# Beginning the first feed-forward group inside the attention's last pair

## The reference, cut to what matters

```python
def _L0_ffn_ref(x, W_fc, W_proj):
    h = jnp.square(jax.nn.relu(jnp.einsum('bsd,fd->bsf', x, W_fc)))
    y = jnp.einsum('bsf,df->bsd', h, W_proj)
    ...   # five steps of a membrane; the spikes are counted
    return jnp.sum(spks, axis=0) / NUM_STEPS
...
x = x + jnp.tanh(g_xattn[0]) * _L0_xattn_ref(ctx_1024, _layernorm(x, axis=-1), mask, ...)
x = x + jnp.tanh(g_ffn[0]) * _L0_ffn_ref(_layernorm(x, axis=-1), L0_ffn_W_fc, L0_ffn_W_proj)
x = x + jnp.tanh(g_xattn[1]) * _L1_xattn_ref(_layernorm(x, axis=-1), ctx_1024, ctx_1024, ...)
x = x + jnp.tanh(g_ffn[1]) * _L1_ffn_ref(_layernorm(x, axis=-1), ...)
```

## Time and profile before

| | |
|---|---|
| three runs | 892.55, 895.89, 898.25 us; median 895.89 |
| the profiled execution | 897.6 us, its span 895.8 us |
| busy in the span: PE, DVE, ACT, POOL | 812.0, 549.6, 368.2, 375.6 us |
| mean granted clock of TensorE | 0.93 of full speed |
| attention's pairs, in the span | from about 105 to 392 us |
| feed-forward up to the last down product | to about 510 us |

### The profile page before, as it was taken

One profiled execution on the slowest core, in us unless ns is written; L12 is line 12 of the kernel. 1 busy time (PEld: TensorE's weight loads), 2 busy tenths in 40 slices (PEclk: granted clock), 3 DMA queues, 4 the chain that ended last, 5 costly groups with the idle time before them and its releaser, 6 DMA issues.

```text
span 895.8 us, 13812 instructions
## 1 busy us (share of the span) xinstructions
PE 812.0 (91%) x4270; PEld 622.5 (69%) x4271; DVE 549.6 (61%) x1173; ACT 368.2 (41%) x1175; POOL 375.6 (42%) x396
## 2 busy tenths in 40 slices
PE   6887799898999899978999889999997799999995
PEld 5555545555555455546888778888886789999994
DVE  4949676767577676457997756777765523333331
ACT  4547134544354333425433177666671022222220
POOL 7355545363546375326433434445443302222221
PEclk9989599998899799987999989999997799999998
DMA  8570000000000000009000091000000384455520
GB/s 302 188 305 1 1 0 1 1 1 1 0 1 1 0 1 1 1 1 356 1 0 1 1 336 59 12 13 13 13 18 21 98 299 166 176 176 175 174 83 2
DMA packets 31886, 67.12 MB, mean 75 GB/s; under 512 B 3103, under 2 KB 22909, under 8 KB 30813
## 3 DMA queue, kind: packets, MB, share of 16 engines
q1 hardware_dynamic: 28699, 56.17, 18.0%
q0 software_dynamic: 2560, 10.17, 3.5%
q10 hardware_dynamic: 578, 0.19, 0.1%
HBM read 54.74 MB, written 12.68 MB: 75 GB/s over the span
## 4 chain that ended last, share of the span: by engine, by line
PE 67%; DVE 17%; issue 7%; ACT 4%; POOL 3%; DMA 2%; DVEq 0%; SPq 0%; ACTq 0%; POOLq 0%
PE PS L2045 9%; PE PS L2033 9%; PE PS L1433 7%; PE PS L727 6%; PE PS L1415 6%; PE PS L1257 4%; PE PS L718 4%; PE PS L694 3%; DVE row_best L835 3%; PE PS L719 3%; PE PS L764 2%; DVE hL L1354 2%; PE PS L736 2%; PE PS L1241 2%; PE PS L747 2%
## 5 line engine op out<-in xcount | busy, mean ns | idle before, releaser
L1027 ACT ACTIVATE EX<-PS 128x512 f32<-128x512 f32 x144 | 79.1, 594 | 139.5 <-PE PS L719 134.2
L835 DVE TENSOR_REDUCE row_best<-PS 128x1 f32<-128x1024 f32 x64 | 77.8, 1221 | 48.8 <-PE PS L694 48.5
L991 POOL TENSOR_TENSOR sumP<-sumP,EX 128x1024 f32<-128x1024 f32 x32 | 75.7, 2366 | 41.8 <-ACT EX L1027 41.3
L2033 PEld LDWEIGHTS PS<-xeT,w 128*128 128x128 f32 x736 | 85.6, 192 | 4.0 <-DMA w<-in_L_ffn_W 1.7
L2033 PE MATMUL PS<-xeT,w 128*128 128x128 f32 x736 | 86.1, 275 | 2.4 <-DMA w<-in_L_ffn_W 1.5
L1615 ACT ACTIVATE pc<-PS,mx 128x77 f32<-128x77 f32 x256 | 78.9, 360 | 21.2 <-DVE mx L1512 21.2
L2045 PE MATMUL PS<-w,heT 128*128 x368 | 83.3, 379 | 1.3 <-DVE oe L1975 1.3
L2072 POOL DMA_INDIRECT out<-oe,target x23 | 23.3, 1011 | 126.0 <-DVE oe L1975 126.0
L727 PE MATMUL PS<-EX,V 128*64 128x512 f32 (+1 forms) x288 | 76.1, 646 | 0.0
L2045 PEld LDWEIGHTS PS<-w,heT 128*128 128x128 f32 x368 | 68.1, 190 | 10.0 <-issue 1.7
L1433 PE MATMUL PS<-vw,pcT 128*128 128x256 f32 (+1 forms) x320 | 72.9, 383 | 1.2 <-ACT pcT L1628 1.2
(11 more groups left out here) (283 smaller groups left out, 1718.0 us busy)
## 6 DMA issues: line engine op xcount, KB each, us to landing
w<-in_L_ffn_W SPq DMA_DIRECT2D x31, 1024.0 KB, 6.5
vw_rows<-vwn SPq DMA_DIRECT2D x2, 1232.0 KB
kwH_rows<-kwH SPq DMA_DIRECT2D x1, 2464.0 KB, 7.4
kwL_rows<-kwL SPq DMA_DIRECT2D x1, 2464.0 KB, 13.7
kwH<-kwH_rows POOLq DMA_DIRECT2D x1, 2464.0 KB, 9.8
kwL<-kwL_rows POOLq DMA_DIRECT2D x1, 2464.0 KB, 16.0
vw<-vw_rows SPq DMA_DIRECT2D x2, 1152.0 KB, 7.3
XR<-in_x SPq DMA_DIRECT2D x4, 512.0 KB, 13.4
```

The costliest lines, as they stand in the source:

```text
L835: dve.tensor_reduce(row_best[:, n % 2, t // GT, t % GT:t % GT + 1], PSf[:, 512 * at:512 * at + S], AX.X, ALU.max, negate=True).then_inc(ma ...
L991: pool.tensor_tensor(sumP[:], before, EX[:, (KT * n + c) % EB, :, :], ALU.add).then_inc(pool_summed, 1)
L1027: act.activation(EX[0:r, k % EB, i, :], PS[0:r, ST_AT + i, :], ACT.Exp).then_inc(exp_done, 1)
L2033: last = pe.matmul(PS[:, 1 + 2 * p + c // 4, c % 4 * P:c % 4 * P + P], w1[:, u, k, c * P:c * P + P], xeT[:, p, k, :], start=k == 0, stop=k ...
```

## The change

The first feed-forward group starts earlier: group 0's statistics go into pair 6 (step 5), its normalization, transposes, copy and low part into pair 7 (steps 2, 4, 4, 5), group 1's statistics, root and normalization into pair 7 too (steps 3, 5, 6). After the last values TensorE goes straight to group 0's up products. Pair 7's sums come after chunk 1, its output products after chunks 3 and 5; VectorE does the reciprocals and additions after the hL of the same chunks. TensorE waits for `proj_added` after chunk 7, GpSimd issues its DMAs after group 0's squares. Group 0 is written out ahead of TensorE's loop, which keeps groups 1 and 2. zTH and zTL lie where wprojT was. The PSUM banks of scores and values are one lower.

Two things change in every pair: `sum_rest` is split, and both halves go into the next pair's step 0, `sum_last` behind `low_parts_of` and `scale_heads` and ahead of `row_max`, `sum_both` behind it; and the second `turn_shift` of step 8 goes between the values of chunks 7 and 8, and behind rows, heads and items in the turn of the spare banks.

```diff
@@ -252,11 +252,13 @@
-    zTH = ffn.take("zTH", [P, KC, GN], F32R)
-    zTL = ffn.take("zTL", [P, KC, GN], F32R)
     relu = ffn.take("relu", [P, 4, GN])
     spikes = ffn.take("spikes", [P, GN])
     assert ffn.at <= CROSS_LOW
+    ffn = Region(TOP - FC * D)
+    zTH = ffn.take("zTH", [P, KC, GN], F32R)
+    zTL = ffn.take("zTL", [P, KC, GN], F32R)
+    assert ffn.at <= TOP
...
     CHUNKS = ((0, 512), (512, 1024))
-    MAX_AT, ST_AT, PV_AT = 0, 3, 5
-    SPARE = (2, 6, 7)
+    MAX_AT, ST_AT, PV_AT = 0, 2, 4
+    SPARE = (5, 6, 7)
+    FFN_AT = dict(stats0=(PP - 2, 5), z0=(PP - 1, 2), stats1=(PP - 1, 3), turn0=(PP - 1, 4), low0=(PP - 1, 5),
+                  root1=(PP - 1, 5), z1=(PP - 1, 6))
+    TAIL_SUM, TAIL_OUT = 1, (3, 5)
     POOL_CHUNKS = 6
...
@@ -807,8 +814,8 @@
                         row_scores(n + 1, c, MAX_AT)
                     if c in (3, 7):
                         ctx_scores(n + 1, c // 4)
-                    if c in (5, 8):
-                        turn_shift(n + 1, (c - 5) // 3)
+                    if c == 5:
+                        turn_shift(n + 1, 0)
...
                 for v, i in items_at(n, c):
                     item(v, i)
+                if (n, c) == FFN_AT["turn0"]:
+                    pe.wait_ge(max_ready, 2 * GT * PP)
+                    ffn_turn(pe, 0)
                 for done in CHUNK_OF_STEP.get(c, ()):
+                    if done == KT - 1 and n + 1 < PP:
+                        turn_shift(n + 1, 1)
                     values(n, done)
-        sums(PP - 1)
-        project_out(PP - 1, 0)
-        project_out(PP - 1, 1)
+        return {TAIL_SUM: lambda: sums(PP - 1), TAIL_OUT[0]: lambda: project_out(PP - 1, 0),
+                TAIL_OUT[1]: lambda: project_out(PP - 1, 1)}
...
-        def sum_rest(n):
+        def sum_last(n):
             dve.wait_ge(exp_done, 2 * (KT * n + KT - 1) + 2)
             dve.wait_ge(dve_summed, 3 * n + 1)
             dve.tensor_tensor(sumD[0:C], sumD[0:C], EX[0:C, (KT * n + KT - 1) % EB, :, :], ALU.add).then_inc(dve_summed, 1)
+
+        def sum_both(n):
             dve.wait_ge(pool_summed, pool_read(n, POOL_CHUNKS - 1))
             dve.wait_ge(dve_summed, 3 * n + 2)
             dve.tensor_tensor(sumD[:], sumD[:], sumP[:], ALU.add).then_inc(dve_summed, 1)
...
+                if n > 0 and c == 0:
+                    sum_last(n - 1)
                 if n + 1 < PP and c < 2 * GT:
                     row_max(n + 1, c, MAX_AT)
+                if n > 0 and c == 0:
+                    sum_both(n - 1)
...
-                if n == PP - 1 and c == 5:
+                if (n, c) == FFN_AT["stats0"]:
                     ffn_stats(dve, 0)
+                if (n, c) == FFN_AT["z0"]:
+                    ffn_z(dve, 0)
+                if (n, c) == FFN_AT["stats1"]:
+                    ffn_stats(dve, 1)
+                if (n, c) == FFN_AT["low0"]:
+                    ffn_z_low(dve, 0)
+                if (n, c) == FFN_AT["z1"]:
+                    ffn_z(dve, 1)
                 if c == KT - 2:
                     sum_first(n)
                 if n + 1 < PP and c == KT - 1:
                     keep_shift(n + 1, 1)
                 for v, i in items_at(n, c):
                     square_sums(v, i)
-            sum_rest(n)
-        ffn_z(dve, 0)
-        reciprocals(PP - 1)
-        add_out(PP - 1, 0)
-        add_out(PP - 1, 1)
+        sum_last(PP - 1)
+        sum_both(PP - 1)
+        return {TAIL_SUM: lambda: reciprocals(PP - 1), TAIL_OUT[0]: lambda: add_out(PP - 1, 0),
+                TAIL_OUT[1]: lambda: add_out(PP - 1, 1)}
 
...
+                if (n, c) == FFN_AT["root1"]:
+                    pool_root(pool, 1)
+            if n == PP - 2:
+                pool_root(pool, 0)
...
+                if (n, c) == FFN_AT["turn0"]:
+                    act.wait_ge(wfc_split, 4)
+                    ffn_copy_turned(act, 0)
...
+    def pe_ffn(pe, tail):
+
+        def group(g, last_group, tail={}):
             pe.wait_ge(g_zT_ready, g + 1)
...
+                if c in tail:
+                    tail[c]()
+            if tail:
+                pe.wait_ge(proj_added, 2 * GT * PP)
             if not last_group:
-                turn(g + 1)
+                ffn_turn(pe, g + 1)
             pe.wait_ge(h_ready, FC * g + FC)
...
-        pe.wait_ge(proj_added, 2 * GT * PP)
         pe.wait_ge(wfc_split, 4)
-        pe.wait_ge(ffn_in, 32)
-        turn(0)
-        with pe.Fori(0, NG - 1) as g:
+        pe.wait_ge(exp_done, 2 * KT * PP)
+        group(0, False, tail)
+        with pe.Fori(1, NG - 1) as g:
             group(g, False)
         group(NG - 1, True)
...
             if not last_group:
-                copy_turned(g + 1)
-        copy_turned(0)
+                ffn_copy_turned(act, g + 1)
         with act.Fori(0, NG - 1) as g:
             group(g, False)
         group(NG - 1, True)
...
         for g in range(NG):
             group(g)
+            if g == 0:
+                pool.wait_ge(proj_added, 2 * GT * PP)
+                pool_refill(pool)
+                for p in range(2):
+                    pool.dma_start(t["mark"][p], iota_low[0:1, 0:P]).then_inc(out_rows[p], 16)
             if g + 2 < NG:
                 pool_root(pool, g + 2)
...
         for g in range(NG - 1):
-            low_parts(g, range(FC))
-            z_low(g + 1)
+            for c in range(FC):
+                low_parts(g, [c])
+                if g == 0 and c in tail:
+                    tail[c]()
+            ffn_z_low(dve, g + 1)
             if g + 2 < NG:
                 ffn_stats(dve, g + 2)
...
         pool_project(pool, 0)
         pool_wfc(pool)
         pool_attend(pool)
-        pool_root(pool, 0)
-        pool_root(pool, 1)
-        pool.wait_ge(proj_added, 2 * GT * PP)
-        pool_refill(pool)
-        for p in range(2):
-            pool.dma_start(t["mark"][p], iota_low[0:1, 0:P]).then_inc(out_rows[p], 16)
         pool_ffn(pool)
         pool_cross(pool)
```

More of the change, by code:

```diff
@@ L652, in spare_uses @@
                     yield "ctx", n + 1, c // 4
-                if n + 1 < PP and c in (5, 8):
-                    yield "shift", n + 1, (c - 5) // 3
+                if n + 1 < PP and c == 5:
+                    yield "shift", n + 1, 0
                 if n > 0 and c == 1:
@@ L665, in spare_uses @@
                     yield "item", v, i
+                if n + 1 < PP and c == 8:
+                    yield "shift", n + 1, 1
         yield "sum", PP - 1, 0
@@ L1221, in layers_kernel, with ffn_turn @@
     EDGES = spike_edges()
-    def pe_ffn(pe):
-        def turn(g):
-            pe.wait_ge(g_z, g + 1)
-            for s in range(GT):
-                for k in range(KC):
-                    last = pe.transpose(PS[:, k, s * P:s * P + P], Z[:, s, k * P:k * P + P], ident[:])
-            last.then_inc(g_zT, 1)
-        def group(g, last_group):
+    def ffn_turn(pe, g):
+        pe.wait_ge(g_z, g + 1)
+        for s in range(GT):
+            for k in range(KC):
+                last = pe.transpose(PS[:, k, s * P:s * P + P], Z[:, s, k * P:k * P + P], ident[:])
+        last.then_inc(g_zT, 1)
+    def pe_ffn(pe, tail):
+        def group(g, last_group, tail={}):
             pe.wait_ge(g_zT_ready, g + 1)
@@ L1259, in group, with ffn_copy_turned @@
                 last.then_inc(y_done, 1)
-        pe.wait_ge(proj_added, 2 * GT * PP)
         pe.wait_ge(wfc_split, 4)
-        pe.wait_ge(ffn_in, 32)
-        turn(0)
-        with pe.Fori(0, NG - 1) as g:
+        pe.wait_ge(exp_done, 2 * KT * PP)
+        group(0, False, tail)
+        with pe.Fori(1, NG - 1) as g:
             group(g, False)
         group(NG - 1, True)
-    def act_ffn(act):
-        def copy_turned(g):
-            act.wait_ge(g_zT, g + 1)
-            for k in range(KC):
-                last = act.activation(zTH[:, k, :], PS[:, k, :], ACT.Copy)
-            last.then_inc(g_zT_ready, 1)
+    def ffn_copy_turned(act, g):
+        act.wait_ge(g_zT, g + 1)
+        for k in range(KC):
+            last = act.activation(zTH[:, k, :], PS[:, k, :], ACT.Copy)
+        last.then_inc(g_zT_ready, 1)
+    def act_ffn(act):
         def group(g, last_group):
@@ L1326, in ffn_z, with ffn_z_low, dve_ffn @@
         last.then_inc(g_z, 1)
-    def dve_ffn(dve):
-        def z_low(g):
-            dve.wait_ge(g_zT_ready, g + 1)
-            for k in range(KC):
-                last = dve.tensor_tensor(zTL[:, k, :], PS[:, k, :], zTH[:, k, :].bitcast(F32), ALU.subtract)
-            last.then_inc(g_zT_low, 1)
+    def ffn_z_low(dve, g):
+        dve.wait_ge(g_zT_ready, g + 1)
+        for k in range(KC):
+            last = dve.tensor_tensor(zTL[:, k, :], PS[:, k, :], zTH[:, k, :].bitcast(F32), ALU.subtract)
+        last.then_inc(g_zT_low, 1)
+    def dve_ffn(dve, tail):
         def spike(g, halves=range(2)):
@@ L1354, in low_parts @@
                 dve.tensor_tensor(hL[:, c, :], square[:, c % 4, :], hH[:, c, :].bitcast(F32), ALU.subtract).then_inc(h_low, 1)
-        z_low(0)
-        ffn_stats(dve, 1)
```

(13 more changed lines are left out.)

## The result

The changed kernel takes 888.2 us (median of 888.6, 888.1, 879.6 and 888.3), the kernel before 897.1 beside it: 0.989 of it, 95% interval 0.984 to 0.994. That is a gain of 8.9 where 22 to 23 were forecast, and the time lies above the range. The profiled execution took 888.6, its span 886.8.

A forecast was written before the change was run, and what follows sets the result against it. TensorE, far ahead in busy time, was taken to lose time idle or at low clock at the seam and starts of pairs 3 and 5. Terms -10.1 - 10.4 - 1.3 = -21.8 took 897.6 to 875.8, median 874.1; range 868 to 883.

The forecast's parts named there:

- (a): Seam between attention and feed-forward: first down product 18.6 us after the last values, for 30.4; 11.8 off.
- the clock's fall once after the sums: Seam: one-column sums expected to lower TensorE's clock once there, a loss of 1.7 us.
- wait for `proj_added` over 0.5: Seam, a sign of the forecast coming true: TensorE would have no such wait.
- the lows of h: Seam: VectorE's hL for eight chunks, 1.25 us each, covered before the down products by only 1.2 us.
- Rival 2: Seam: VectorE bounds group 0, so the seam gives 5.4 us for 10.1; time 879; chance 10%.
- (b): Work moved into pairs 6 and 7: transposes +1.0, statistics +0.4, normalization 0.3 (between 0 and 2.4); together +1.7 us.
- (c): Starts of pairs 3 and 5: keys' low parts ahead of both sums remove the gap; 5.2 us each, 10.4 together.
- (e): Second sum behind the row maximum at the other pair starts: together 0 us, between -1 and +3.
- rival 3: Pair starts: second sum behind the maximum lengthens idle, clock falls at every start; slower, 903; chance 3%.
- rival 1: Starts of pairs 3 and 5: the clock does not come back, 2.2 us for 10.4; time 882; chance 10%.
- (d): Shift's product behind the first values: chunk 7's values run in TensorE's waits for NM and the bank; 1.3 us saved.

The follow-up runs named there:

- z0_early: Changed kernel with group 0's normalization in pair 7's step 0 in place of step 2: 883.9 us, ratio 0.983.
- seam_only: Changed kernel with VectorE's order and the shift at the pair starts put back as before, seam and moved work kept: 887.2 us, ratio 0.987.
- wide_values: z0_wide with chunk 0's values ahead of the sums: 861.6 us, ratio 0.960.
- z0_seam: seam_only with group 0's normalization in pair 7's step 0: 883.7 us, ratio 0.984.
- both_first: Changed kernel with the second sum ahead of the row maximum again, both sums still behind the keys' low parts: 886.1 us, ratio 0.989.
- z0_both: both_first with group 0's normalization in pair 7's step 0: 884.1 us, ratio 0.984.
- z0_wide: z0_early with the sums' products 64 columns wide in place of one: 873.4 us, ratio 0.974.
- before_wide: Kernel before the change with the sums' products 64 columns wide, nothing else: 885.2 us, ratio 0.988.
- z0_values: z0_early with chunk 0's values ahead of the sums, one-column products kept: 869.3 us, ratio 0.966.
- seam_values: z0_seam with chunk 0's values ahead of the sums, old order at the pair starts: 886.4 us, ratio 0.989.
- wide_values_noshift: wide_values with the shift's product where it was before the change: 860.9 us, ratio 0.960.

## Why the prediction missed

**Seam (a): right, mis-sized by 1.7.** 30.44 came to 16.93, a gain of 13.5 for 11.8. (I put two output products at 2.0 together; the halves that I named make 1.85, and they took 1.13 each.) The 1.7 was the clock's fall once after the sums; with up products on both sides the clock stayed at 1.00. No wait for `proj_added` over 0.5 appeared (0.38), and the lows of h were no bound: they take 0.69 one at a time, between GpSimd's squares, not the 1.25 I carried over from a row of eight. Rival 2 is out.

**Moved work (b): the normalization was mis-sized.** I took 0.3 between 0 and 2.4; it was 2.4 of waiting and 1.7 of clock, 4.1, and 4.3 by `z0_early`. The bound from the rows was the right wait but left out what a wait costs in clock. The rule of the Trainium skill that I had weighed ("SBUF — State Buffer", "Who interferes with whom") agrees with the 5.83 us row: the operations ended with GpSimd's additions. I chose against it because TensorE had a step between, without laying the additions of pair 7 beside the moved operations, where two more of them were due. The errors of (a) and (b), -1.7 and +3.8, cancel in part, by luck: -13.5 + 1.0 + 0.4 + 4.1 = -8.0 by the changed kernel's trace, for -10.1 forecast. `seam_only` measured -9.2 to -11.3; its trace lacks the wait of 2.4.

**Starts of pairs 3 and 5 (c): right where nothing else is late.** The gaps of 2.29 and 2.43 are gone. The new order, worth 10.4 by the forecast, is worth 13.5 in `wide_values` and 17.0 with one-column products and the values first. In the changed kernel it was worth nothing (883.9 against 883.7 in `z0_early` and `z0_seam`).

**The second sum behind the maximum (e): the step that failed.** I put it at 0, between -1 and +3, counting the waits alone, and those were right: 3.0 in six places. What I did not count is what a wait of 0.5 does to the clock when one-column products follow. In the profiled execution the stretches at 1.2 GHz grew at pairs 1, 2 and 6, stayed at 6.8 and 10.1 at pairs 3 and 5, and over all seven starts they sum to 44.2, for 44.5 before. Filling the wait brought 14.6, so by that edit the term is about +15 and not 0. With it and the other terms as forecast the sum is -10.1 - 10.4 - 1.3 + 14.6 = -7.2, for 8.9 measured. The split between (c) and (e) is mine and not measured: the second sum put back ahead of the maximum (`both_first`, `z0_both`) returns 2 us or nothing, for then TensorE waits for the maximum, 12.9 in place of 6.1. What is shown is the pair of them: 10.4 forecast, 0 found, and 17.0 once chunk 0's values stand ahead of the sums. Nor does the wait cost the same each time: at pair 4 the clock stayed at 1.00 behind 0.49 of it.

This is rival 3's mechanism, which I gave 3%. I had it decide only where further falls cost more than all the rest gained, and had no case between: the falls eat (c) and the seam's gain stays. Part of rival 1 is in it too, since the clock at pairs 3 and 5 did not come back (0.60 and 0.61); its rule of the Trainium skill ("TensorE: Matmul & The Clock Gate", "What's actually happening"), that sustained activity lifts the clock, agrees with the rows in this: at the start of pair 3 two waits and sixteen one-column products from 224.88 to 228.36, and 1.2 GHz behind them. That the one-column products weigh in this is shown by `z0_wide` and `before_wide`; that the wait does, by `z0_values` with `seam_values` beside it: the same edit brings 14.6 where it fills a wait and nothing where there is none.

**The shift (d): -1.3 forecast, none measured.** The waits for NM fell from 4.4 to 2.4, but those of the key products for the kept shift rose from 0.5 to 3.5 on the weight loads' queue. The wait changed its owner. Without the move, `wide_values_noshift` is as fast.

**What stays open.** From the start of pair 1 to that of pair 7 the changed kernel took 2.4 us longer in the two profiled executions (134.94 to 370.57, before 133.59 to 366.85: 235.6 for 233.3). The gaps (-4.7) and the waits for the second sum (+3.0) make -1.7, the clock at the first six starts changed by (44.2 - 41.1) / 2 = +1.6, and the statistics add +0.4; that leaves 2.1 without an owner; the new waits for the kept shift may be some of it, which is not shown. Which wait costs the clock, that for the maximum or that for the second sum, is not separated. Why executions of one kernel differ by 9 us and more in how often their clock falls is not explained either.

## What to carry to other kernels

Count TensorE's waits twice: once as time, and once for the clock behind them, above all where one-column products follow a wait; filling six waits of 0.5 us brought 14.6 here. When you trade one order on a shared engine for another, put something that is ready, here 1 us of 512-column products, between TensorE and the result that it still waits for. Neither was worth anything without the other here: the order alone 0, the values first alone 0, both together 14.4. So test such a pair of edits in all four combinations. When a short operation of VectorE moves, lay GpSimd's long ones beside its new place.
